# Node stage of a graph-attention and expert kernel: the turning of a block's rows moved between the two halves of the previous block's products, and a subtraction moved ahead of the next block's relu

## The reference, cut to what matters

```python
out = out.reshape(N, H * C) + bias
return jax.nn.relu(out)
...
x = x + _L0_gnn_ref(_layernorm(x, axis=-1), edge_index, ...)
... _layernorm(x, axis=-1)[None] ...
proj = jnp.einsum('bsd,ed->bse', x, Wp)
pn = _l2norm(proj)
gate_scores = jnp.einsum('bsd,ed->bse', pn, sn) / temperature
```

## Time and profile before

| what | value |
|---|---|
| median of 3 runs | 2454.21 us (2448.95 to 2456.05) |
| the profiled execution, its own time | 2455.99 us |
| its span, first to last instruction | 2454.2 us |
| around the span | 1.8 us |
| busy in the span | PE 82%, DVE 62%, ACT 45%, POOL 29% |
| mean granted TensorE clock | 0.903 of full speed |
| the node stage | about 1370 to 1664 us of the span |

### The profile page before, as it was taken

One profiled execution on the slowest core, in us unless ns is written; L12 is line 12 of the kernel. 1 busy time (PEld: TensorE's weight loads), 2 busy tenths in 40 slices (PEclk: granted clock), 3 DMA queues, 4 the chain that ended last, 5 costly groups with the idle time before them and its releaser, 6 DMA issues. The chain is left out here.

```text
span 2454.2 us, 53610 instructions
## 1 busy us (share of the span) xinstructions
PE 2006.4 (82%) x14842; PEld 1337.3 (54%) x14843; DVE 1517.5 (62%) x4463; ACT 1115.4 (45%) x2399; POOL 709.3 (29%) x933
## 2 busy tenths in 40 slices
PE   2888897666669999999999387773898999999997
PEld 1455555444438787878888255442344444444553
DVE  3776674777767777777777678877533433433332
ACT  2333432111128787878787355541533433433332
POOL 0002000000016666666665001001222332333332
PEclk9899898555689999999999689995899999999999
DMA  3533344233019999999999455545545546545442
GB/s 131 170 101 112 111 140 138 97 129 123 0 56 353 363 343 362 346 348 354 344 354 333 150 180 184 184 149 189 222 166 215 216 149 216 202 159 168 162 170 80
DMA packets 141057, 489.14 MB, mean 199 GB/s; under 512 B 22449, under 2 KB 22659, under 8 KB 138829
## 3 DMA queue, kind: packets, MB, share of 16 engines
q0 software_dynamic: 98912, 346.99, 40.3%
q1 hardware_dynamic: 41853, 140.70, 15.9%
q10 hardware_dynamic: 216, 0.43, 0.0%
HBM read 418.06 MB, written 81.27 MB: 203 GB/s over the span
## 5 line engine op out<-in xcount | busy, mean ns | idle before, releaser
L1035 PE MATMUL main_ps<-rows,O 128*128 128x256 f16 x4992 | 576.5, 274 | 49.7 <-DVE acc L974 28.6
L1021 ACT ACTIVATE O<-O,pk 128x128 f16<-128x128 f16 x1664 | 499.5, 387 | 126.0 <-DVE O L991 124.3
L1035 PEld LDWEIGHTS main_ps<-rows,O 128*128 128x128 f16 x4992 | 463.7, 98 | 120.1 <-DVE acc L974 33.7
L960 POOL DMA_INDIRECT rows<-projected,idx x416 | 394.6, 948 | 199.5 <-issue 83.7
L1744 PE MATMUL pj_ps<-gram,xsT 128*125 128x512 f16 x1200 | 292.6, 405 | 46.0 <-ACT xsT L396 45.3
L995 DVE TENSOR_SCALAR O<-O,pk 128x128 f16<-128x128 f16 x1664 | 319.2, 270 | 14.9 <-DVE O L991 0.2
L1695 PE MATMUL x_h<-w_p,gram 128*128 x1344 | 309.1, 388 | 17.1 <-ACT gram L1648 11.3
L1710 PE MATMUL x_o<-w_p,gram 128*128 x1344 | 310.8, 382 | 1.4 <-ACT gram L1664 1.4
L1744 PEld LDWEIGHTS pj_ps<-gram,xsT 128*125 128x125 f16 x1200 | 171.0, 146 | 155.8 <-ACT xsT L396 53.5
L1695 PEld LDWEIGHTS x_h<-w_p,gram 128*128 128x128 f16 x1344 | 132.3, 100 | 171.9 <-issue 33.2
L1753 PE MATMUL n_pj<-gram,PK 128*128 128x512 f16 (+3 forms) x900 | 166.5, 344 | 62.1 <-ACT PK L1226 62.1
(11 more groups left out here) (332 smaller groups left out, 2619.2 us busy)
## 6 DMA issues: line engine op xcount, KB each, us to landing
w_f<-in_L_ffn_W_dram SPq DMA_DIRECT2D x14, 2048.0 KB, 12.9
b_t<-in_L_ffn_b_dram SPq DMA_DIRECT2D x56, 512.0 KB, 4.7
xt<-in_x_dram SPq DMA_DIRECT2D x25, 500.0 KB
projected_f<-xp_f POOLq DMA_DIRECT2D x25, 500.0 KB, 3.7
projected<-xp POOLq DMA_DIRECT2D x25, 500.0 KB, 4.8
n_own<-projected_f SPq DMA_DIRECT2D x25, 500.0 KB
n_xt<-in_x_dram SPq DMA_DIRECT2D x25, 500.0 KB
out_dram<-n_x POOLq DMA_DIRECT2D x25, 500.0 KB, 9.9
```

Source lines behind the costliest of these rows:

```text
L960: pool.indirect_dma_start(out=rows[:, 4 * p + k, :, :].rearrange("k n d -> k (n d)"), out_offset=None, in_=xp_d[:, :], in_offset=bass.Indi ...
L1021: ins = act.activation(O[:, k, 1 + HEADS + h, :], O[:, k, 0, :], ACT.Copy, scale=pk[:, p, k, w:w + 1])
L1035: pe.matmul(main_ps[:, h * C:(h + 1) * C], O[:, k, 1 + HEADS * a + h, :], rows[:, 4 * p + k, b, h * C:(h + 1) * C], start=first and h % 2 ...
```

## The change

The low half of block i now comes ahead of the relu step of block i + 1 on DVE; the lengths and scores run two blocks behind instead of one, so `xn` gets a third buffer; and PE turns block i + 1 between the scores and half 1 of block i's products.

```diff
-                xn = sbuf(c, "n_xn", [ROWS, 2, D])
+                xn = sbuf(c, "n_xn", [ROWS, 3, D])
...
                             near(dve.tensor_tensor(own[:, p, :], x2[:, p, :], bias_b[:, :], ALU.add))
+
+                        def relu_and_add(i):
+                            p = i % 2
+                            dve.wait_ge(s_x2c, 2 * i + 2)
                             dve.scalar_tensor_tensor(x2[:, p, :], own[:, p, :], 0.0, xt[:, p, :], ALU.max, ALU.add).then_inc(s_x2, 1)
...
                         layer_out(0)
+                        relu_and_add(0)
                         moments(0)
                         for i in range(BLOCKS):
                             inverse_std(i)
...
                                 layer_out(i + 1)
                             low(i)
                             if i + 1 < BLOCKS:
+                                relu_and_add(i + 1)
                                 moments(i + 1)
-                            if i >= 1:
-                                length_and_scores(i - 1)
-                        length_and_scores(BLOCKS - 1)
+                            if i >= 2:
+                                length_and_scores(i - 2)
+                        for i in (BLOCKS - 2, BLOCKS - 1):
+                            length_and_scores(i)
...
+                            if i >= 3:
+                                act.wait_ge(s_sc, i - 2)
                             if i >= 2:
-                                act.wait_ge(s_sc, i - 1)
                                 act.wait_ge(s_tr, i - 1)
                                 act.wait_ge(s_xo[p], 16 * (i // 2))
-                            act.activation(xn[:, p, :], x2[:, p, :], ACT.Identity, bias=ln[:, p, 8:9], scale=ln[:, p, 7:8])
+                            act.activation(xn[:, i % 3, :], x2[:, p, :], ACT.Identity, bias=ln[:, p, 8:9], scale=ln[:, p, 7:8])
...
-                        for i in range(BLOCKS):
-                            p = i % 2
+                        def turn(i):
                             pe.wait_ge(s_xn, i + 1)
                             if i >= 1:
                                 pe.wait_ge(s_xnT, i)
-                            turn_parts(pe, tr_ps, xs[:, p, :, :], ident16).then_inc(s_tr, 1)
+                            turn_parts(pe, tr_ps, xs[:, i % 2, :, :], ident16).then_inc(s_tr, 1)
+                        turn(0)
+                        for i in range(BLOCKS):
+                            p = i % 2
                             pe.wait_ge(s_xnT, i + 1)
                             if i >= 2:
                                 pe.wait_ge(s_sc, i - 1)
                             lhs = xsT[:, p, :, :, :]
                             triangle(pe, pj_ps[:, p, :], lhs, gram, 0, range(KD // 2))
                             product(pe, sc_ps[:, p, 0:WIDE], lhs, sim_wide, range(KD), KD)
+                            if i + 1 < BLOCKS:
+                                turn(i + 1)
                             triangle(pe, pj_ps[:, p, :], lhs, gram, 1, range(KD)).then_inc(s_mm, 1)
```

More of the change, by code:

```diff
@@ L1173, in low @@
                             dve.wait_ge(s_xh, i + 1)
-                            dve.tensor_tensor(xs[:, p, 1, :], xn[:, p, :], xs[:, p, 0, :], ALU.subtract).then_inc(s_xn, 1)
+                            dve.tensor_tensor(xs[:, p, 1, :], xn[:, i % 3, :], xs[:, p, 0, :], ALU.subtract).then_inc(s_xn, 1)
                         def length_and_scores(i):
@@ L1178, in length_and_scores @@
                             dve.wait_ge(s_mm, i + 1)
-                            dve.scalar_tensor_tensor(pj_ps[0:ROWS, p, :], pj_ps[0:ROWS, p, :], 1.0 / WS, xn[:, p, :], ALU.mult, ALU.mult,
+                            dve.scalar_tensor_tensor(pj_ps[0:ROWS, p, :], pj_ps[0:ROWS, p, :], 1.0 / WS, xn[:, i % 3, :], ALU.mult, ALU.mult,
                                                      accum_out=nsq[:, i:i + 1])
```

## The result

The changed kernel took 2463.3 us, median of 13 runs (2454.4 to 2478.3); the kernel before took 2453.0 us beside it (13 runs, 2446.8 to 2456.1). The ratio is **1.0053, 95% interval 1.0037 to 1.0069**: slower by some 13 us by the ratio and by 10.3 us by the medians, where no change was forecast as the likeliest and 2451 us as the time. The profiled execution took 2464.1 us, its span is 2462.3.

The account below looks back on a forecast made before the run. It took the node stage to be bound by the turn of landing, scaling, copy, relu, issue and load: 9.92 + 13.43 - 1.2 = 22.15 us. That gains 3 us over 22 blocks, plus 1 at the end: 2451 us, range 2443 to 2465.

Parts of the forecast that it names:

- What bounds the stage: Node stage: the loop from a load's landing through ACT and DVE to the next issue sets the pace, 22.43 us per two blocks.
- Transposes between the halves: PE order: removing its 10.16 us chain, under 11.21 a block, saves only the copy's 0.22 us a turn.
- The sign given for it: PE's wait for the copy falls under 15 us; a low-half wait of about 2.5 us a block replaces it.
- The relu ends 1.14 us later, landing to issue 9.92 us: DVE order: the low half ahead of the relu delays SP's load issue, costing 0.92 us a turn, 0.46 a block.
- slower rival: Stores gain nothing between loads and the later issue is paid in full: 2465 us; slower 0.23 in all, clock included.
- The stores move too: POOL's halves' store goes 0.85 us before the load's issue, saving 1.2 us a turn, bounds 0 and 1.55.
- the hole: Idle gap on the five load engines between one load and the next, about 1.5 us for stores to use.
- The last blocks: Last two blocks, no load in the way: the new order gains between 0 and 1.5 us, taken as 1.
- TensorE's clock: PE's waits might lower its clock: nothing for one stretch; about 2540 us if low for whole blocks, chance 2%.
- The price of at most 1.6 us on half 1: PE: one low-clock stretch costs half 1 at most 1.6 us of 2.6 that are free, so nothing.
- the prediction's stretch of 3.3 us at the full clock: PE before the change: a quiet 3.3 us of wait and transposes kept the full clock in the trace.

## Why the prediction was wrong, by its own steps

- **What bounds the stage** held. A turn of landing, scaling, copy, relu, issue and landing sets the pace in both kernels: cutting the load alone took 21 us off the stage, and with it the order of the transposes, worth nothing before, was worth 18.9.
- **Transposes between the halves, worth nothing by themselves**, held: 0.9989. The sign given for it did not: PE's wait for the copy, forecast under 15 us, is 39.2 in the changed kernel, where the blocks swing, and 2.4 with the relu first. ACT's wait for loads, forecast at 80 to 100 us, is 119.6.
- **The relu ends 1.14 us later, landing to issue 9.92 us** held: 9.92. With both stores behind the load a block took 11.64 and 11.65 us; the slower rival had 11.68.
- **"The stores move too" failed.** It took 1.2 us off each load, from 13.43 to 12.2, because the five engines would do the stores' work in the hole. Measured was 13.97 and 14.52, so 0.6 to 1.15 us more than before's 13.37. The work in the hole was done, but the load's first byte was held fixed at 1.7 us after its issue, an estimate that no row showed. The runs show 0.9 with the queue empty and the stores behind, and no sooner than 2.3, then at half rate, with the halves' store ahead. The load gives back at its start what the hole gained: 13.56 us with that store alone ahead, against 13.31 with both behind. The rest, up to 13.97 and 14.52, came only with both stores early, in blocks that fall into pairs, where the next block's stores reach over a load's end. The term left those out, and why the pairs arise is open. Without the term the prediction's own sum is a loss of 9 us; with it, a gain of 4. Its bounds were wrong too: 0 stood as the lowest saving with no reason that excluded a cost.
- **The slower rival** had the right mechanism for half of the loss: its 9 us (10.2 less 1) stand against 8.7 us of stage with both stores behind the load, and against 17.8 in the changed kernel. Its 2465 us lies close to the measured 2463.3, in part by luck: it knew nothing of the second half, it was reckoned from the profiled 2456.0 where the median before is 2453.0, and the time grew by less than the stage.
- **The last blocks**: from block 24's scaling to the last length 29.8 us against 30.3, a gain of 0.5 against 1 forecast.
- **TensorE's clock** set nothing, but it did fall. The mean granted clock was 0.903 in both executions. PE waited 2.5 us ahead of the transposes in six blocks of the changed kernel. Once the products behind them ran in the 4.38 us of the full 2.4 GHz level; in the other five they took 1.3 to 1.7 us more, at the 1.2 GHz level in part. Shown are one block of either kind, then a block after a short wait, and the window that goes with the second (columns as in rows 4):

```profile
1404.17 1.05 PE L1774 MATMUL n_tr<-ident,PK 125*128 125x125 f16 x16 [2.50 <-DVE PK L1178]
1405.06 4.38 PE L1765 MATMUL n_pj<-gram,PK 128*128 128x512 f16 x24
...
1463.98 1.05 PE L1774 MATMUL n_tr<-ident,PK 125*128 125x125 f16 x16 [2.51 <-DVE PK L1178]
1464.87 7.70 PE L1765 MATMUL n_pj<-gram,PK 128*128 128x512 f16 x36
...
1583.94 6.01 PE L1765 MATMUL n_pj<-gram,PK 128*128 128x512 f16 x36
...
1465.20:1468.00 2.80, 2.80 (x8) 0.98 (x7) 2.73 (x7) 2.58 (x5) 0.52 (x1) 0.50 0.95 230
```

  The price of at most 1.6 us on half 1 was about right, and it cost the pace nothing that can be seen, as the prediction said: PE still waited for the next low half. So the prediction's stretch of 3.3 us at the full clock does not carry over to the longer one of wait and transposes here.

## What to carry to other kernels

Before an operation is moved ahead of another, look at what the delayed one releases on SP and POOL. Here 1.14 us on VectorE delayed a load's issue and moved two stores to its front. The later issue and the stores each cost some 9 us of stage by the profiles, 5 and 8 us by the times. The wait that looks largest on TensorE was worth nothing until the load was short, and then 19 us of stage. For a term that no row shows, keep a cost as well as a gain in its bounds, and ask for its start as well as its volume.

## What the runs showed of the hardware that was not expected

- A load on an idle queue moves its first bytes 0.9 us after its issue. A store issued 0.87 us ahead of it puts them off to some 2.4 us; meanwhile the DMA engines, at 93%, move 229 GB/s.
- Two stores early together cost 8 to 12 us in the stage with TensorE's new order; either alone cost under 2.
- SP's issue of a whole `xt` takes 1.06 to 1.41 us in the mean instead of 0.34 to 0.37 where the halves' store goes out 0.87 us ahead of the load; in one kernel this cost next to nothing.
- Cutting 125 rows into 112 and 13 took a load from 14.0 us or more to 9.4 in the order of the change, and from 13.4 to 8.6 in the order of before.
